# Rows stored twice normalised, and one accumulation group for the second expert layer

## What is computed

```python
x = _layernorm(x + _L0_attn_ref(x, guidance))          # attention over 8 differences, 64 guide vectors
x = _layernorm(x + _L0_ffn_ref(x, Wr, br, ln_g, ln_b, W1, b1, W2, b2))
# _L0_ffn_ref, for the chosen one of 8 experts:
router_probs = softmax(xt @ Wr + br); gates = max(router_probs); idx = argmax(router_probs)
xn = (xt - mean(xt)) * rsqrt(var(xt) + LN_EPS) * ln_g + ln_b
y = (relu(xn @ W1[idx] + b1[idx]) @ W2[idx] + b2[idx]) * gates
```

## Time and profile before

| | |
|---|---|
| median of 3 runs | 201.93 us (200.13 to 201.94) |
| the profiled execution's own time | 202.25 us |
| its span in the trace | 200.5 us |
| busy share of the span | DVE 80%, PE 74%, ACT 74%, PEld 59%, POOL 57% |
| mean granted TensorE clock | 0.908 |

### The profile page before, as it was taken

How to read it: one execution, slowest core, us unless ns; L and a number is a source line. 1 busy time by engine, 2 the same in 40 slices (tenths; PEclk the granted TensorE clock), 3 DMA queues, 4 the chain that set the end, 5 groups by cost and what they waited for, 6 DMA issues and landing times.

```text
span 200.5 us, 5489 instructions
## 1 busy us (share of the span) xinstructions
PE 147.8 (74%) x1446; PEld 118.1 (59%) x1446; DVE 161.1 (80%) x819; ACT 148.1 (74%) x448; POOL 114.3 (57%) x200
## 2 busy tenths in 40 slices
PE   0068979988997795922369878998998997999400
PEld 0015736857566474821316767987888996888200
DVE  2455287999998869699698899999999999799900
ACT  2358979997975696527645887999999999898520
POOL 4323140508789765634469215768677687578650
PEclk9999999999999998585556999999999999999955
DMA  5997184000101101101342212223222222110000
GB/s 131 346 394 261 26 273 159 3 0 15 40 26 35 42 29 41 54 15 40 77 126 83 56 30 55 66 71 76 65 75 64 66 64 69 53 54 19 28 9 0
DMA packets 16415, 15.74 MB, mean 79 GB/s; under 512 B 2810, under 2 KB 13142, under 8 KB 16386
## 3 DMA queue, kind: packets, MB, share of 16 engines
q1 hardware_dynamic: 14034, 11.10, 19.0%
q0 software_dynamic: 2272, 4.27, 6.4%
q10 hardware_dynamic: 80, 0.03, 0.1%
HBM read 10.52 MB, written 5.33 MB: 79 GB/s over the span
## 4 chain that ended last, share of the span: by engine, by line
PE 43%; DVE 33%; issue 8%; ACT 6%; DMA 3%; ACTq 2%; POOLq 1%; SPq 1%; POOL 0%; DVEq 0%
PE bank L473 7%; DVE hl L1239 6%; PE bank L592 6%; PE bank L430 5%; PE bank L445 4%; DMA XN<-in_attn_embeddings 3%; DVE z L1248 3%; PE bank L502 3%; PE bank L580 3%; PE bank L576 2%; PE bank L578 2%; DVE zpart L1244 2%; PE bank L579 2%; PE bank L595 2%; DVE bn L1252 2%
## 5 line engine op out<-in xcount | busy, mean ns | idle before, releaser
L418 POOL DMA_INDIRECT out<-OUT,tok x39 | 40.5, 1039 | 26.5 <-issue 25.0
L383 POOL DMA_INDIRECT rows<-R,place x32 | 31.8, 994 | 18.0 <-DVE place L919 9.4
L592 PE MATMUL bank<-W2hl,hh 128*128 x156 | 32.6, 274 | 7.0 <-issue 3.2
L576 PE MATMUL bank<-sel,bias 96*128 96x128 bf16 x156 | 34.6, 222 | 0.0
L578 PE MATMUL bank<-xh,W1h 128*128 128x128 f16 x156 | 34.2, 219 | 0.0
L580 PE MATMUL bank<-xh,W1l 128*128 128x128 f16 x156 | 34.1, 218 | 0.0
L579 PE MATMUL bank<-xl,W1h 128*128 128x128 f16 x156 | 34.0, 218 | 0.0
L1239 DVE SCALAR_TENSOR_TENSOR hl<-bank,hh 128x512 f16<-128x512 f32 x39 | 26.9, 690 | 3.5 <-ACT hh L746 2.6
L595 PE MATMUL bank<-W2hl,hl 128*128 x156 | 27.9, 219 | 0.0
L746 ACT ACTIVATE hh<-bank 128x512 f16<-128x512 f32 x39 | 23.1, 593 | 6.1 <-PE bank L580 5.8
L359 POOL TENSOR_TENSOR rmag<-guarded,minus_half 128x4 f32<-128x4 f32 x8 | 8.2, 1022 | 27.0 <-ACT guarded L615 27.0
(11 more groups left out here) (197 smaller groups left out, 459.3 us busy)
## 6 DMA issues: line engine op xcount, KB each, us to landing
XR<-rows SPq DMA_DIRECT2D x39, 66.0 KB
W<-in_ffn_W SPq DMA_DIRECT2D x1, 2048.0 KB, 11.0
X<-in_attn_embeddings SPq DMA_DIRECT2D x2, 512.0 KB, 8.6
X<-in_attn_embeddings SPq DMA_DIRECT2D x1, 768.0 KB
out<-OUT,tok POOLq DMA_INDIRECT x39
rows<-padt SPq DMA_DIRECT2D x9, 66.0 KB
XN<-in_attn_embeddings SPq DMA_DIRECT2D x2, 256.0 KB, 7.9
rows<-R,place POOLq DMA_INDIRECT x32
```

The costliest lines, as they stand in the source:

```text
L383: pool.indirect_dma_start(out=rows[:, :], out_offset=bass.IndirectOffsetOnAxis(ap=place[u][:, k:k + 1], axis=0), in_=R[u][:, k, :], in_off ...
L418: pool.indirect_dma_start(out=out[:, :], out_offset=bass.IndirectOffsetOnAxis(ap=tok[k][:, 0:1], axis=0), in_=OUT[k][:, :], in_offset=None ...
L576: pe.matmul(h, bias3[:, c * P:(c + 1) * P], sel, start=True, stop=False)
L592: pe.matmul(y[:, 0:2 * D], hh[k][:, c * P:(c + 1) * P], w, start=c == 0, stop=False)
```

## The change

Rows are scattered as xn without gain and shift (scaled with r1), not x1. Since layer norm with a scaled epsilon undoes a scale of the whole row, the last norm is made on f (x1 + gate y): column D now holds f / sum(exp), column D + 1 the scaled epsilon f^2 eps, which enters `b_sd` as the bias of the square root. The router's logits, formed from xn, are multiplied by r0/r1 (`VP`) before the bias is added. `b_xs` is gone: TensorE transposes `XR` itself. Layer two issues high times high and high times low as two matmuls of 128 columns into the same 128 columns of PSUM, so `z` is one operation. `cg` moves from GpSimd to VectorE, two turns ahead. GpSimd copies columns D + 1 and D + 2 together into `tok`; `b_hh` no longer waits for it, `b_sd` does.

```diff
@@ scatter
-                pool.wait_ge(s["both"], 2 * u + 2)
+                pool.wait_ge(s["both"], 3 * u + 3)
@@ SP load
-                after(sp, every["z0"], blocks(count(-1), k))
+                after(sp, every["z"], blocks(count(-1), k))
@@ token (GpSimd)
-                pool.tensor_scalar(cg[k][:, :], XR[k][:, D:D + 1], scl[:, 3:4], None, ALU.mult)
-                pool.tensor_copy(tok[k][:, :], XR[k][:, D + 2:D + 3].bitcast(I32)).then_inc(every["token"], 1)
+                pool.tensor_copy(tok[k][:, :], XR[k][:, D + 1:D + 3].bitcast(I32)).then_inc(every["token"], 1)
@@ b_xT (TensorE)
-                pe.wait_ge(every["xs"], blocks(count(0), k))
-                pe.transpose(bank[7 * (k % 2)][:, 0:P], xs[k][:, :], ident).then_inc(every["xT_ps"], 1)
+                pe.wait_ge(row_loaded[k], count(1) * 16)
+                after(pe, every["xt"], blocks(count(0), k) - 2)
+                pe.transpose(bank[7 * (k % 2)][:, 0:P], XR[k][:, 0:D], ident).then_inc(every["xT_ps"], 1)
@@ b_y (TensorE)
-                    pe.matmul(y[:, 0:2 * D], hh[k][:, c * P:(c + 1) * P], w, start=c == 0, stop=False)
+                    pe.matmul(y[:, 0:D], hh[k][:, c * P:(c + 1) * P], wh, start=c == 0, stop=False)
+                    pe.matmul(y[:, 0:D], hh[k][:, c * P:(c + 1) * P], wl, start=False, stop=False)
@@ x1 (ScalarE)
-                                       scale=rstd[u % 2][:, 0, k:k + 1], bias=st[u % 3][:, WR, k:k + 1])
+                                       scale=rstd[u % 2][:, 1, k:k + 1], bias=st[u % 3][:, WR, k:k + 1])
@@ ScalarE stages
-                act.activation(xs[k][:, :], XR[k][:, 0:D], ACT.Identity, scale=XR[k][:, D + 1:D + 2]).then_inc(every["xs"], 1)
-                act.wait_ge(every["token"], blocks(count(0), k))      # in b_hh
+                act.wait_ge(every["token"], blocks(count(0), k))      # in b_sd
-                act.activation(sd[k][:, 0:1], mv2[k][:, 1:2], ACT.Sqrt, bias=epsc[:, 0:1]).then_inc(every["sd"], 1)
+                act.activation(sd[k][:, 0:1], mv2[k][:, 1:2], ACT.Sqrt, bias=tok[k][:, 0:1].bitcast(F32)).then_inc(every["sd"], 1)
-            steps([(5, b_xs), (1, b_hh), (-3, b_fin), (4, b_xt), (-2, b_sd), (4, b_xh)])
+            steps([(1, b_hh), (-3, b_fin), (4, b_xt), (-2, b_sd), (4, b_xh)])
@@ window: do_g, after L889
-                    dve.reciprocal(R[g][:, :, D], rt[:, 2, :])
+                    dve.reciprocal(rt[:, 2, :], rt[:, 2, :]).then_inc(s["esum"], 1)
+                    tt(R[g][:, :, D], R[g][:, :, D], rt[:, 2, :], ALU.mult)
@@ window: do_r (a multiplication at L953, the addition of the bias ahead of L972)
-                    tt(lg[:, :, :], log_ps[...], by_expert(brb[:, :]), ALU.add).then_inc(s["lgs"], 1)
+                    tt(lg[:, :, :], log_ps[...], by_tile(st[r % 3][:, VP, :]), ALU.mult).then_inc(s["lgs"], 1)
+                    tt(lg[:, :, :], lg[:, :, :], by_expert(brb[:, :]), ALU.add).then_inc(s["lgs"], 1)
@@ window: do_y, at its end
-                    tt(R[y][:, :, D + 1], sy[:, RV, :], vars_[y % 2][:, 0, :], ALU.mult).then_inc(s["both"], 1)
+                    tt(R[y][:, :, D], sy[:, RV, :], vars_[y % 2][:, 0, :], ALU.mult).then_inc(s["both"], 1)
+                    tt(sy[:, VP, :], sy[:, RV, :], vars_[y % 2][:, 1, :], ALU.mult)
+                    dve.wait_ge(s["both"], 3 * y + 2)
+                    stt(R[y][:, :, D + 1], R[y][:, :, D], LN_EPS, R[y][:, :, D], ALU.mult, ALU.mult).then_inc(s["both"], 1)
@@ VectorE stages
-                stt(z0[k][:, :], bank[5 + k % 2][:, 0:D], cg[k][:, :], XR[k][:, 0:D], ALU.mult, ALU.add).then_inc(every["z0"], 1)
-                stt(z[k][:, :], bank[5 + k % 2][:, D:2 * D], cg[k][:, :], z0[k][:, :], ALU.mult, ALU.add).then_inc(every["z"], 1)
+                ts(cg[k][:, :], XR[k][:, D:D + 1], scl[:, 3:4], None, ALU.mult).then_inc(every["cg"], 1)
+                stt(z[k][:, :], bank[5 + k % 2][:, 0:D], cg[k][:, :], XR[k][:, 0:D], ALU.mult, ALU.add).then_inc(every["z"], 1)
-            steps([(1, b_hl), (-1, b_mv), (0, b_z0), (-2, b_rec), (0, b_z), (-2, b_shift), (0, b_bn), (0, b_table), (4, b_xl), (4, b_split)])
+            steps([(1, b_hl), (-1, b_mv), (-2, b_rec), (0, b_z), (2, b_cg), (-2, b_shift), (0, b_bn), (0, b_table), (4, b_xl), (4, b_split)])
```

More of the change, by code:

```diff
@@ L183, in build @@
         XR = [sb(f"XR{i}", [P, ROW]) for i in range(UN)]
-        tok = [sb(f"tok{i}", [P, 1], I32) for i in range(UN)]
-        xs = [sb(f"xs{i}", [P, D]) for i in range(UN)]
+        tok = [sb(f"tok{i}", [P, 2], I32) for i in range(UN)]
         cg = [sb(f"cg{i}", [P, 1]) for i in range(UN)]
@@ L191, in build @@
         hl = [sb(f"hl{i}", [P, FF], F16) for i in range(UN)]
-        z0 = [sb(f"zpart{i}", [P, D]) for i in range(UN)]
         z = [sb(f"z{i}", [P, D]) for i in range(UN)]
@@ L209, in build @@
         padded = sem("padded")
-        every = {n: sem("every_" + n) for n in "token xs xh xl hl z xT_ps xt h_ps hh y_ps z0 bn mv sd rec shift out".split()}
+        every = {n: sem("every_" + n) for n in "token cg xh xl hl z xT_ps xt h_ps hh y_ps bn mv sd rec shift out".split()}
         seen = sem("seen")
@@ L418, in store @@
                 pool.indirect_dma_start(
-                    out=out[:, :], out_offset=bass.IndirectOffsetOnAxis(ap=tok[k][:, 0:1], axis=0),
+                    out=out[:, :], out_offset=bass.IndirectOffsetOnAxis(ap=tok[k][:, 1:2], axis=0),
                     in_=OUT[k][:, :], in_offset=None, bounds_check=T - 1, oob_is_err=False).then_inc(stored[k], 16)
@@ L590, in b_y @@
                 for c in range(FC):
-                    w, wh = W2hl[:, bass.ds(e, 1), c, :], W2hl[:, bass.ds(e, 1), c, 0:D]
-                    pe.matmul(y[:, 0:2 * D], hh[k][:, c * P:(c + 1) * P], w, start=c == 0, stop=False)
+                    wh, wl = (W2hl[:, bass.ds(e, 1), c, part * D:(part + 1) * D] for part in range(2))
+                    pe.matmul(y[:, 0:D], hh[k][:, c * P:(c + 1) * P], wh, start=c == 0, stop=False)
+                    pe.matmul(y[:, 0:D], hh[k][:, c * P:(c + 1) * P], wl, start=False, stop=False)
                     if c == 0:
@@ L952, in window @@
                         dve.wait_ge(ld["small"], 32)
-                    tt(lg[:, :, :], log_ps[:, 0:NT * E].rearrange("p (k e) -> p k e", k=NT), by_expert(brb[:, :]), ALU.add).then_inc(s["lgs"], 1)
+                    dve.wait_ge(s["both"], 3 * r + 3)
+                    tt(lg[:, :, :], log_ps[:, 0:NT * E].rearrange("p (k e) -> p k e", k=NT), by_tile(st[r % 3][:, VP, :]), ALU.mult).then_inc(s["lgs"], 1)
                 if do_y and i >= NU:
@@ L1239, in b_hl, with b_cg, b_z @@
                 stt(hl[k][:, :], bank[1 + k % 4][:, :], 0.0, hh[k][:, :], ALU.max, ALU.subtract).then_inc(every["hl"], 1)
-            def b_z0(count, k):
+            def b_cg(count, k):
+                dve.wait_ge(row_loaded[k], count(1) * 16)
+                ts(cg[k][:, :], XR[k][:, D:D + 1], scl[:, 3:4], None, ALU.mult).then_inc(every["cg"], 1)
+            def b_z(count, k):
+                dve.wait_ge(every["cg"], blocks(count(0), k))
                 dve.wait_ge(every["y_ps"], blocks(count(0), k))
-                stt(z0[k][:, :], bank[5 + k % 2][:, 0:D], cg[k][:, :], XR[k][:, 0:D], ALU.mult, ALU.add).then_inc(every["z0"], 1)
-            def b_z(count, k):
-                dve.wait_ge(every["z0"], blocks(count(0), k))
-                stt(z[k][:, :], bank[5 + k % 2][:, D:2 * D], cg[k][:, :], z0[k][:, :], ALU.mult, ALU.add).then_inc(every["z"], 1)
+                stt(z[k][:, :], bank[5 + k % 2][:, 0:D], cg[k][:, :], XR[k][:, 0:D], ALU.mult, ALU.add).then_inc(every["z"], 1)
             def b_bn(count, k):
```

17 lines of the change are left out of this document (10 added, 7 removed).

## The result

The changed kernel takes 215.31 us in the median of 4 runs (214.82 to 217.82), the kernel before 201.76 (200.13 to 201.94, 4 runs). The ratio is 1.0716, with a 95% interval of 1.0616 to 1.0816. The forecast was 198.9, its range 196.2 to 202.6: the sign was wrong, and the time lies outside. The profiled execution took 214.82 us, its span is 213.0.

What follows compares the result with a forecast made beforehand. Blocks were taken as bound by ScalarE at 1.88 us, VectorE and TensorE close behind, dense windows by VectorE. Blocks 10 to 38 -2.9, blocks 0 to 10 -1.6, end -0.3, windows +1.8: 201.93 to 198.9 us, range 196.2 to 202.6.

Steps and rivals of the forecast that it cites:

- TensorE's floor: Blocks: layer two goes from 9 matmuls in 0.73 us to 13 in 0.74, so TensorE needs 1.75 a block.
- the 1.74: Blocks: TensorE's time for one block right after a stall, 137.37 to 139.11, read as what it can do.
- Both cost nothing: Blocks: the transpose's later waits for row and xt, and row loads issued some 0.2 us later, add no time.
- VectorE and ScalarE: Blocks: without zpart but with cg VectorE's period falls to 1.69 us; without xs ScalarE's falls to 1.58.
- The wait for sd: Blocks: VectorE's reciprocal waits 0.1 to 0.2 us for ScalarE's sd, period about 1.75 to 1.8 unless hl slides back.
- rival 1: Blocks: VectorE's new wait for sd, not TensorE, holds a block at 1.82 or so; 201.0 us, 16 in 100.
- the stalls for expert numbers: Blocks 10 to 38: TensorE's reads cost 2.4 us plus 0.5 for waits on hl; costing nothing, 3.8 saved.
- Rival 2: Windows: the clock falls a window earlier, 2.5 to 5 us more, half the blocks' gain; 204.5 us, 9 in 100.
- The windows: Four more VectorE operations a window, 0.45 us in a full one, add 1.8 us in sum, bounds 0.8 and 3.3.
- Rival 3: Windows: the clock holds longer, 79 to 85 us at 2.4 GHz, some 2.5 us less; 196.4 us, 10 in 100.
- The end: After the blocks: the last z no longer follows zpart, saving 0.3 us, bounds 0 and 0.4.
- Rival 5: Blocks: pairs cost the same at 256 columns as at 128, TensorE at 1.97 a block; 206.2 us, 2 in 100.

Runs made afterwards that it cites:

- experiment 2: Changed kernel with layer two reading expert 0's weights at a fixed address, its 13 matmuls kept: 198.84 us, ratio 0.9747.
- experiment 7: Kernel before with hl times the low instead of the high half of layer two's weights, four more register instructions a block, no more matmuls: 209.45 us, ratio 1.0403.
- experiment 9: Changed kernel with the transpose's wait for xt moved to a matmul of layer one that had none: 211.32 us, ratio 1.0537.
- experiment 10: Changed kernel with layer two's 256-column matmul and two halves back, cg on GpSimd, the transpose's xt wait moved to layer one: 203.32 us, ratio 1.0143.
- experiment 8: Kernel before with only the change's four more VectorE operations in each window, blocks untouched: 203.75 us, ratio 1.0141.
- 4: Kernel before with layer two's 256-column matmul split into two of 128 columns, still into two separate halves: 211.49 us, ratio 1.0361.
- 3: Changed kernel with layer two's order in a chunk altered to high times high, low times high, high times low: 217.19 us.
- 5: Changed kernel with W2's halves in two tiles, so layer two's eight fused register instructions become eight additions: 213.65 us, ratio 1.0643.
- 6: Changed kernel with layer one reading expert 0's weights at a fixed address, layer two unaltered: 200.98 us in one run.
- 11: Changed kernel with both layers reading expert 0's weights at fixed addresses: 195.67 us in one run.
- experiment 1: Changed kernel with layer two's 256-column matmul into two halves, zpart and z put back as before: 209.95 us, ratio 1.0244.

## Why the prediction was wrong

**The step that failed** is TensorE's floor: "So 13 cost 0.74, and the floor becomes 1.75", with bounds "nothing, if only columns count, and 4 × 0.057 = 0.23 if a pair costs the same however wide". The 13 do cost 0.73 (experiment 2). But neither bound has a term for what stands in TensorE's stream and leaves no row in the timeline, the address of each new operand. The change doubles layer two's from four to eight, each 0.124 us of the sequencer: 0.50 us more, of which 0.17 (1.74 less 1.57) were free. The price is 0.19 us a block beyond the slack, by experiment 7; the separate wait adds 0.12, from 2.20 against 2.08 (experiment 9). 1.88 + 0.19 + 0.12 = 2.19, where 2.20 was measured. Over blocks 10 to 38: 54.78 + 5.94 (experiment 7) + 3.20 (experiment 9) = 63.9, measured 64.13.

**What the 1.74 was.** I took 1.74 us, one block right after a stall, for TensorE's floor, and counted 0.14 us of slack. It was right for the stream that I read it from, and no lead made it look too short. The stall is the read of expert numbers, which holds the sequencer itself (a TENSOR_LOAD of 0.72 us at 136.09, and no register instruction starts before 136.87): after it layer two's first register instruction starts 0.10 us ahead of its matmul, as in the steady blocks, and 1.75 us later 0.35 ahead. Experiment 10, with the same 12 instructions, has three such blocks in a row (1.75, 1.74, 1.74), while experiment 7 takes 2.12 and the changed kernel 2.33 right after that stall. What failed is to carry the figure to a stream with five instructions more. The source said the rest: layer two's four wide matmuls share their address with the four narrow ones, and the split gives each chunk an address more.

**"Both cost nothing"**, of the transpose's new waits, failed too. Neither is ever late, as I argued, but two of them are one instruction more, 0.11 to 0.12 us a block, 3.2 us over blocks 10 to 38.

**VectorE and ScalarE** were right in so far as both keep up with a block of 1.75 in experiment 2, with ScalarE busy 9.76 of 10 us. Their own periods, 1.69 and 1.58, show in no run, since TensorE leads wherever their work is that of the change. The wait for sd is there as well, in the changed kernel and in experiment 2 (VectorE's timeline of experiment 2):

```profile
144.46 0.17 DVE L1263 BATCH_NORM_AGGREGATE mv<-bn 128x2 f32<-128x6 f32 x1
144.67 0.16 DVE L1267 RECIPROCAL sd<-sd 128x1 f32<-128x1 f32 x1
144.77 0.35 DVE L1253 SCALAR_TENSOR_TENSOR z<-bank,cg,XR 128x128 f32<-128x128 f32 x1
```

From mv to the reciprocal are 0.21 us, 0.13 more than the 0.08 of a step without a wait; 0.1 to 0.2 was foreseen. It does not hold the block at 1.82, so rival 1 falls. Experiment 2's gain over blocks 10 to 38 is 5.1 us, where I had 2.9 and a best bound of 3.8: the stalls for expert numbers, for which I kept 2.9 us, cost 0.65 there (49.65 less 28 × 1.75). A part of that bound was a wrong sum: with no stall costing anything 54.8 less 49.0 is 5.8, not 3.8. Rival 2's time is one too: 4 us and half of the blocks' gain, 2.25, on top of 198.9 make some 205.2, not 204.5. Neither touches the step that failed.

**The windows** were put at +1.8 us, with bounds of 0.8 and 3.3. The change cost 1.4 up to the first layer two, experiment 8 2.4 in the median. VectorE's first operations of windows 4 and 5 are 9.01 us apart, not 9.2 (beside the earlier trace rows):

```profile
40.25 0.23 DVE L801 RECIPROCAL st<-bank 128x2 f32<-128x2 f32 x2
...
49.26 0.23 DVE L801 RECIPROCAL st<-bank 128x2 f32<-128x2 f32 x2
```

So 0.26 for a full window, not 0.45. Profiles scatter by more than the term, though. The first layer two starts at 111.94, 113.69 and 112.28 with the windows of before (before, 4, 7). With those of the change it starts between 112.90 and 115.96 in nine profiles (after, 2, 3, 5, 6, 8 to 11) and at 119.83 in experiment 1. The medians are 112.3 and 114.0, 1.8 apart, but the 1.4 of the single pair is no confirmation, and a part of the agreement is luck.

Rival 2's mechanism, time at the lower clock ahead of 75 us, is there, but not as its own terms have it. The changed kernel has 0.90 from 50 to 80 us instead of 0.97. Experiment 7 has 0.90 with the windows of before, and experiments 2, 3, 5 and 6 have 1.00 with those of the change, so the runs do not show that the four operations bring it about. It is dear in experiment 1 alone. Rival 3 falls: the stretch from 80 to 109 us has a granted clock of 0.56 as before. The end gave the 0.3 us that were foreseen.

Where the prediction and experiment 8's expectation write 2.4 or 1.2 GHz, the traces show a granted clock of 1.00 or 0.50. In the kernel before, matmuls of 512 columns on ones (L430) start 0.215 us apart at 44.48 us, at a granted clock of 1.00, and 0.427 apart at 105.85, at 0.50. As an estimate from these, that is 2.4 and 1.2 columns a ns, and the two figures stand for no more than that here.

**Rival 5** has the nearest time, 206.2, and a wrong reason: it makes four more pairs dear, and experiment 7 pays the same without them. A pair of weight load and 128-column matmul takes 57 ns in whole blocks with fixed addresses in layer two or in both (experiments 2 and 11), and 73 in the mean over the changed kernel's block (2.20 over 30). I was right on the price of the pair, and wrong to leave it at that instead of asking what else stands between the pairs of this stream.

## What to carry to other kernels

Where TensorE is near the bound, here 0.14 us below it, count its instruction list and not only its matmuls: in these runs each new address from a register, and the second wait of the transpose, took a place in the stream, 0.11 to 0.13 us. By the estimate of the table 12 of them, 1.44 us, cost nothing beside 1.74 of matmuls, and 16, 1.94, made a block 2.07. Cutting a matmul in two cost the second address, though the columns stayed the same and the four matmuls more were nearly free (2.08 in experiment 4, 2.07 in experiment 7). And a floor read from a stretch of the trace is that of the instruction stream of that stretch: 1.74 with 12 such instructions was not the floor with 17, which took 2.20.

## What the runs showed of the hardware

- Register instructions in TensorE's stream, which the timeline leaves out, take 0.124 us of its sequencer as FUSED_REGOPS, 0.113 as ALU_OP; a separate wait takes 0.126 (records of the changed kernel). They run beside the matmuls: 12 in a block cost nothing (1.74 us after the stall in the kernel before), 16 make it 2.07 (experiment 7).
- Where they stand mattered: nine in a block of 30 matmuls cost nothing with eight of them in layer one (1.75 us, experiment 2) and 0.14 us with eight in layer two (1.89, experiment 6).
- In layer two of the changed kernel each shows as a gap of 0.11 or 0.13 us between weight loads (162.60 to 162.84); of two in a chunk only the second shows between matmuls (0.12 instead of 0.06).
- A read of expert numbers costs a block 0.09 and 0.11 us (the first two after block 10) where the sequencer has a lead of 0.9 us (1.84 and 1.86 against 1.75, experiment 2), and 0.87 and 0.98 where it has none (3.07 and 3.18 against 2.20, the changed kernel).
- A pair of weight load and 128-column matmul every 57 ns holds over whole blocks, with all loads overlapped (1.75 us for 29 and a transpose, experiments 2 and 11).
- The granted clock from 50 to 80 us differs between profiles of the same windows: 0.97, 1.00 and 0.90 with those of before (before, 4, 7), 0.83 to 1.00 with those of the change.
